# Cross-attention and router FFN on one core: where scores and transposed probabilities stand in PSUM, and the order of a slot's work

## The reference, cut to what matters

```python
def attention(query, key, value, position_ids, mask, Wq, Wk, Wv, Wo):   # 32 batches of 64 rows, E = 512
    q = (query @ Wq)  # 32 heads of D = 128
    k = (key @ Wk)    # 8 key/value heads, each for 4 heads of q
    v = (value @ Wv)
    q, k = rope(q), rope(k)
    scores = where(mask == 0, -1e9, q @ k.T / sqrt(D))
    return (softmax(scores) @ v) @ Wo

def ffn(x, weight, bias, gate_w, in_channel_scale, out_channel_scale):
    routing = softmax(x @ gate_w.T)
    return x * (routing @ in_channel_scale) @ sign(weight).T * (routing @ out_channel_scale) + bias

x = x + attention(layernorm(x), ctx, ctx, pos, mask, Wq, Wk, Wv, Wo)
x = x + ffn(layernorm(x), ...)
```

## Time and profile before

| | us |
|---|---|
| median of 3 runs (1306.85 to 1307.28) | 1307.17 |
| the profiled execution | 1309.06 |
| its span | 1307.2 |
| PE busy | 1192.8 (91%) |
| DVE busy | 842.7 (64%) |
| POOL busy | 722.0 (55%) |
| ACT busy | 554.0 (42%) |
| mean granted clock of PE | 0.978 |

### The profile page before, as it was taken

How to read it: one execution, slowest core, us unless ns; L and a number is a source line. 1 busy time by engine, 2 the same in 40 slices (tenths; PEclk the granted TensorE clock), 3 DMA queues, 4 the chain that set the end, 5 groups by cost and what they waited for, 6 DMA issues and landing times.

```text
span 1307.2 us, 23826 instructions
## 1 busy us (share of the span) xinstructions
PE 1192.8 (91%) x7636; PEld 957.9 (73%) x7636; DVE 842.7 (64%) x1367; ACT 554.0 (42%) x1768; POOL 722.0 (55%) x593
## 2 busy tenths in 40 slices
PE   5799999999999999998999999999999999999977
PEld 4577777777777777776777777777777777777755
DVE  6667666666676666666666666656666666666644
ACT  3344444444434444443444444444444354344422
POOL 4566654554665554655455665545565655565424
PEclk8799999999999999999999999999999999999977
DMA  8233332222322222332322322323222222232100
GB/s 212 66 101 101 92 95 77 80 76 75 110 82 73 72 80 64 115 95 86 87 63 65 97 75 77 96 62 101 81 82 80 66 72 64 72 89 73 57 1 33
DMA packets 136924, 106.04 MB, mean 81 GB/s; under 512 B 12776, under 2 KB 111080, under 8 KB 136864
## 3 DMA queue, kind: packets, MB, share of 16 engines
q1 hardware_dynamic: 131488, 94.78, 25.0%
q10 hardware_dynamic: 4608, 8.39, 1.9%
q0 software_dynamic: 768, 2.10, 0.5%
HBM read 101.05 MB, written 4.19 MB: 81 GB/s over the span
## 4 chain that ended last, share of the span: by engine, by line
PE 66%; DVE 15%; ACT 7%; issue 7%; POOL 2%; ACTq 1%; DMA 1%; SPq 1%; DVEq 1%; POOLq 0%
PE chunk L1001 18%; PE chunk L1003 16%; PE chunk L1002 16%; ACT probs L529 5%; PE o_ps L1073 5%; PE sc_ps L1048 4%; PE tr_ps L990 3%; DVE scores L724 2%; DVE oT_lo L707 2%; DVE neg_max L729 1%; DVE acc L714 1%; DVE f_tile L813 1%; PE aux L1151 1%; DVE swp L773 1%; POOL y L430 1%
## 5 line engine op out<-in xcount | busy, mean ns | idle before, releaser
L396 POOL TENSOR_TENSOR w_lo<-raw,w_hi 128x512 fp32r<-128x512 f32 x192 | 256.6, 1343 | 473.1 <-ACT w_hi L495 472.6
L773 DVE TENSOR_TENSOR swp<-chunk,sinT 64x512 f32<-64x512 f32 x320 | 220.3, 689 | 42.6 <-PE chunk L1003 37.5
L529 ACT ACTIVATE probs<-scores,neg_max 128x64 f32<-128x64 f32 x512 | 171.0, 335 | 149.6 <-DVE neg_max L729 149.6
L1001 PE MATMUL chunk<-wo_hi,oT_hi 128*128 128x512 f32 x512 | 210.2, 411 | 1.8 <-issue 1.8
L1001 PE MATMUL chunk<-xT_hi,w_hi 128*128 128x512 f32 (+1 forms) x512 | 208.2, 407 | 0.2 <-DVE kT L775 0.2
L1003 PE MATMUL chunk<-wo_hi,oT_lo 128*128 128x512 f32 x512 | 201.6, 394 | 0.0
L1002 PE MATMUL chunk<-wo_lo,oT_hi 128*128 128x512 f32 x512 | 201.1, 393 | 0.0
L1002 PE MATMUL chunk<-xT_lo,w_hi 128*128 128x512 f32 (+1 forms) x512 | 200.9, 392 | 0.0
L1003 PE MATMUL chunk<-xT_hi,w_lo 128*128 128x512 f32 (+1 forms) x512 | 200.3, 391 | 0.0
L403 POOL TENSOR_TENSOR qT<-qT,swp 128x512 f32<-128x512 f32 x128 | 165.9, 1296 | 46.8 <-DVE qT L775 46.8
L396 POOL TENSOR_TENSOR wo_lo<-raw,wo_hi 128x512 fp32r<-128x512 f32 x132 | 170.2, 1290 | 20.6 <-ACT wo_hi L495 20.6
(11 more groups left out here) (266 smaller groups left out, 2005.2 us busy)
## 6 DMA issues: line engine op xcount, KB each, us to landing
raw<-in_L_xattn_Wo SPq DMA_DIRECT2D x132, 256.0 KB, 2.6
raw<-in_L_xattn_Wq SPq DMA_DIRECT2D x128, 256.0 KB, 2.7
raw<-in_L_xattn_Wk SPq DMA_DIRECT2D x32, 256.0 KB
raw<-in_L_xattn_Wv SPq DMA_DIRECT2D x32, 256.0 KB
acc<-in_x ACTq DMA_DIRECT2D x16, 256.0 KB, 2.8
c_tile<-in_ctx SPq DMA_DIRECT2D x12, 256.0 KB, 3.0
x_tile<-in_x SPq DMA_DIRECT2D x12, 256.0 KB, 3.5
result<-y ACTq DMA_DIRECT2D x12, 256.0 KB, 2.1
```

The source lines that it names most:

```text
L396: nc.gpsimd.tensor_tensor(lo, raw[:, n % RING, :], hi.bitcast(F32), ALU.subtract).then_inc(wsplit_lo, 1)
L529: last = nc.scalar.activation(probs[:, d, bass.ts(k, S)], scores[:, 2 * d + k // 4, bass.ts(k % 4, S)], ACT.Exp, bias=neg_max[:, d, k:k + ...
L773: last = nc.vector.tensor_tensor(swp[to, k, :], bank[of, :], sinT[to, here], ALU.mult)
L1001: nc.tensor.matmul(bank, a_hi, b_hi, start=i == 0, stop=False)
```

## The change

- PSUM: duo 0 has `sc_ps` for its scores and then for its transposed probabilities, duo 1 has `tr_ps` in the same way (`DUO_BANK`). V's transposes go to the first bank of `o_ps` (`V_BANK`), the transposed rope rows to the second (`TABLE_BANK`) in place of `aux`.
- Waits of PE: `v_rows` waits for the last `out_lo` of the slot before (was: the last `pT_lo_split`). `scores_of(s, d)` waits for the slot before's `pT_lo_split` of the same duo (was: the `soft_a` before it). `probs_T` waits only for its own probabilities. `values(s, 0)` now waits for `v_ok` and, in an intake slot, `rope_ok`; `values(s, 1)` waits for the two `out_lo` of `values(s, 0)` as before. `t_rows` no longer waits for `c_lo`; `t_x` waits for `c_lo` in place of `rope_ok`.
- PE's order in a slot: out_proj 0, v_rows, scores 0, scores 1, (t_context, t_f), out_proj 1, 2, 3, project 0, probs_T 0, probs_T 1, (t_rows, t_x, t_logits), project 1, values 0, (t_route), project 2, (t_in_scales), project 3, (t_out_scales), values 1, project 4, (t_product), project 5.
- The orders of ACT, DVE and POOL are rewritten to fit. No instruction is added or removed, and none changes its shape.

```diff
+        DUO_BANK, V_BANK, TABLE_BANK = [sc_ps, tr_ps], o_ps[0], o_ps[1]
...
(POOL, slot)
                 if s.proj:
                     rope_sum(s, 0)
+                    rope_sum(s, 1)
                     split_lo(s, 5)
                     split_lo(s, 6)
-                    rope_sum(s, 1)
                     split_lo(s, 7)
                     rope_sum(s, 2)
                 if s.ffn:
                     xs_lo_split(f[0], in_slot)
                 if s.proj:
+                    rope_sum(s, 3)
                     split_lo(s, 8)
-                    rope_sum(s, 3)
                     split_lo(s, 9)
                     rope_sum(s, 4)
...
(ACT, slot: a residual load, the store and the ends are as before)
-                if s.attn:
-                    v_in_rows(s)
                 if s.proj and not s.first_proj:
                     split_hi(s, 0)
                     split_hi(s, 1)
+                if s.attn:
+                    v_in_rows(s)
+                if s.proj:
+                    split_hi(s, 2)
                 if s.intake:
                     c_split(*t)
+                if s.ffn:
+                    f_transposed(f[0], in_slot)
                 if s.attn:
                     exp_duo(s, 0)
-                if s.proj:
-                    split_hi(s, 2)
+                    exp_duo(s, 1)
+                    pT_hi_split(s, 0)
                 if s.intake:
                     rope_tables(*t)
-                if s.ffn:
-                    f_transposed(f[0], in_slot)
-                if s.attn:
-                    exp_duo(s, 1)
-                if s.intake:
                     x_split(*t)
-                if s.attn:
-                    pT_hi_split(s, 0)
                 if s.ffn:
                     router_exp(f[0], in_slot)
-                if s.attn:
-                    pT_hi_split(s, 1)
+                if s.proj:
+                    split_hi(s, 3)
+                    split_hi(s, 4)
                 if s.number == SLOTS:
                     for n in range(HG):
                         split_hi(s, n)
-                if s.proj:
-                    split_hi(s, 3)
-                    split_hi(s, 4)
-                if s.attn:
+                if s.attn:
+                    pT_hi_split(s, 1)
                     out_hi(s, 0)
                     out_hi(s, 1)
...
                 if s.proj:
                     split_hi(s, 5)
                     split_hi(s, 6)
-                if s.attn:
-                    out_hi(s, 2)
-                    out_hi(s, 3)
-                if s.proj:
                     split_hi(s, 7)
...
                 if s.ffn:
                     xs_split(f[0], in_slot)
+                if s.attn:
+                    out_hi(s, 2)
+                    out_hi(s, 3)
+                if s.ffn:
                     out_scales(f[0], in_slot)
...
(DVE, slot, as it reads now)
+                    f_norm(*f, in_slot)
                 if s.wo:
                     add_out(s, 0)
                 if s.attn:
                     v_lo_split(s)
+                    soft_a(s, 0)
+                    soft_a(s, 1)
                 if s.intake:
+                    c_lo_split(*t)
                     x_norm(t[0])
                 if s.wo:
                     add_out(s, 1)
                 if s.attn:
                     soft_b(s, 0)
                 if s.wo:
                     add_out(s, 2)
+                    add_out(s, 3)
+                if s.attn:
+                    soft_b(s, 1)
...
+                if s.proj:
+                    rotate(s, 0)
+                if s.ffn:
+                    router_max(f[0], in_slot)
+                if s.attn:
+                    pT_lo_split(s, 0)
                 if s.intake:
                     x_lo_split(*t)
                 if s.ffn:
                     routing(f[0], in_slot)
+                if s.proj:
+                    rotate(s, 1)
                 if s.attn:
                     pT_lo_split(s, 1)
+                if s.ffn:
+                    route_lo(f[0], in_slot)
+                if s.attn:
                     out_lo(s, 0)
                     out_lo(s, 1)
                 if s.proj:
+                    rotate(s, 2)
+                if s.ffn:
+                    scale_in(f[0], in_slot)
...
+                if s.proj:
+                    rotate(s, 3)
                 if s.attn:
                     out_lo(s, 2)
                     out_lo(s, 3)
...
(PE, waits)
                 pe.wait_ge(vT_ok, s.U)
                 if not s.first_attn:
-                    pe.wait_ge(pT_l, (s.U - 1) * DUOS)
+                    pe.wait_ge(o_lo, (s.U - 1) * PAIRS)
...
                 pe.wait_ge(roped, s.U * KQ)
-                if not (s.first_attn and d == 0):
-                    pe.wait_ge(masked, n)
+                if not s.first_attn:
+                    pe.wait_ge(pT_l, n - DUOS + 1)
...
                 if d == 0:
                     pe.wait_ge(v_ok, s.U)
+                    if s.intake:
+                        pe.wait_ge(rope_ok, jobs_of(s)[0][0] + 1)
                 else:
                     pe.wait_ge(o_lo, 2 * n)
```

More of the change, by code:

```diff
@@ L867, in slot @@
                     add_out(s, 2)
-                if s.attn:
-                    soft_a(s, 1)
-                if s.intake:
-                    x_lo_split(*t)
-                if s.wo:
                     add_out(s, 3)
                 if s.attn:
-                    pT_lo_split(s, 0)
-                if s.ffn:
-                    router_max(f[0], in_slot)
-                if s.attn:
                     soft_b(s, 1)
-                if s.ffn:
-                    routing(f[0], in_slot)
                 if s.first_proj:
@@ L890, in slot @@
                 if s.proj:
-                    rotate(s, 1)
-                if s.ffn:
-                    route_lo(f[0], in_slot)
-                if s.attn:
-                    out_lo(s, 2)
-                    out_lo(s, 3)
+                    rotate(s, 2)
                 if s.ffn:
                     scale_in(f[0], in_slot)
-                if s.proj:
-                    rotate(s, 2)
                 if s.first_proj:
@@ L904, in slot @@
                     rotate(s, 3)
+                if s.attn:
+                    out_lo(s, 2)
+                    out_lo(s, 3)
                 if s.ffn:
@@ L1047, in scores_of @@
                                 queries = slice(at * P + a * S, at * P + (a + 1) * S)
-                                last = nc.tensor.matmul(sc_ps[a * S:(a + 1) * S, bass.ts(place, S)],
+                                last = nc.tensor.matmul(DUO_BANK[d][a * S:(a + 1) * S, bass.ts(place, S)],
                                                         qT[:, hp, queries], kT[:, bass.ts(at, S)], start=True, stop=True)
@@ L1066, in values @@
                 pe.wait_ge(pT_l, n + 1)
-                if not (s.first_attn and d == 0):
+                if d == 0:
+                    pe.wait_ge(v_ok, s.U)
+                    if s.intake:
+                        pe.wait_ge(rope_ok, jobs_of(s)[0][0] + 1)
+                else:
                     pe.wait_ge(o_lo, 2 * n)
@@ L1166, in slot @@
                     scores_of(s, 0)
+                    scores_of(s, 1)
                 if s.intake:
                     t_context(t)
-                if s.wo:
-                    out_proj(s, 1)
-                if s.intake:
-                    t_rows(t)
                 if s.ffn:
@@ L1175, in slot @@
                 if s.wo:
+                    out_proj(s, 1)
                     out_proj(s, 2)
-                if s.attn:
-                    scores_of(s, 1)
-                if s.intake:
-                    t_x(t)
-                if s.wo:
                     out_proj(s, 3)
+                if s.proj:
+                    project(s, 0)
                 if s.attn:
                     probs_T(s, 0)
+                    probs_T(s, 1)
+                if s.intake:
+                    t_rows(t)
+                    t_x(t)
                 if s.ffn:
@@ L1187, in slot @@
                 if s.proj:
-                    project(s, 0)
+                    project(s, 1)
                 if s.attn:
-                    probs_T(s, 1)
                     values(s, 0)
-                if s.proj:
-                    project(s, 1)
                 if s.ffn:
                     t_route(f, in_slot)
-                if s.attn:
-                    values(s, 1)
                 if s.proj:
@@ L1207, in slot @@
                     t_out_scales(f, in_slot)
+                if s.attn:
+                    values(s, 1)
                 if s.proj:
```

43 lines of the change are left out of this document (18 added, 25 removed).

## The result

The changed kernel takes 1205.8 us (median of 4 runs, 1205.16 to 1207.55), the kernel before 1307.22 in the same comparison (1306.85 to 1307.34). The ratio is 0.9227, with a 95% interval of 0.9211 to 0.9243: 101.4 us less. The forecast was 1213.5, with a range of 1203 to 1245. The profiled execution took 1205.52, its span is 1203.7 us, the mean granted clock 0.989.

The account below looks back on a forecast made before the run. PE was taken as the bound. Slot gains of 85.2 us plus 3.0 and 5.5 at the ends, 93.7 in all, took the profiled 1309.06 to 1215.4, less 1.9 to the median: 1213.5 us, range 1203 to 1245.

Parts of the forecast that it names:

- The bound: Whole kernel: PE, busy 1192.8 of 1307.2 us, sets the end; the change can gain only where PE stands idle.
- The layout of a slot: Table of starts in a slot on all engines: 33.3 us plain, 34.2 intake, with 0.4 to 2.2 us spare at seams.
- Rival (a): POOL bounds a slot, its eight late instructions taking 1.50 us instead of 1.27: 29 us in all, 1242 us; chance 7%.
- each group of small matmuls costs 0.25 us beyond its own work: On PE between wide blocks: 0.17 us in the first wide block after, some 0.08 at the step to small.
- 0.37 + 1.23 + 0.25: Plain slot's gain: waits for soft_b and out_lo gone, one small-matmul group fewer; 1.85 us, with 2.0 taken.
- Intake: Twelve intake slots: waits for soft_b, out_lo and small ones go, two groups fewer; 3.6 us each, 43.2 in all.
- Slots 1 and 32: The ends: some waits stay; gains of 3.0 us (0 to 5) in slot 1, 5.5 (3 to 6) from slot 32.
- (b): values 0 waits in place of values 1, about 0.8 us in each of 30 slots: 24 us, 1237 us; chance 9%.
- (c): PE's clock falls once per slot in the longer small-matmul stretch, 1.7 us each: 51 us, 1265 us; chance 5%.
- (d): The clock fall in the small-matmul stretch lasts, 7 us a slot: 112 us, 1326 us, slower than before; chance 3%.

Follow-up runs that it names:

- one more group: The changed kernel with probs_T(s, 0) ahead of project(s, 0), so one more group of transposes stands between wide blocks: 1206.93 us, ratio 0.9223.
- `scale_in` first: The changed kernel with scale_in ahead of rotate(s, 2) on DVE in FFN slots: 1200.47 us, ratio 0.9173.
- `pT_lo_split(s, 0)` late: The changed kernel with pT_lo_split(s, 0) behind rotate(s, 1) on DVE: 1338.75 us, ratio 1.0236.

## Why the prediction was right, and where its terms were off

**The bound.** Right. PE's line set the end before and after, and what was gained is PE's time: 114 - 40 = 74 us of idle time, the other 29 overlap, steps between shapes and clock.

**The layout of a slot.** It held to some tenths. `pT_lo_split(s, 0)` ends 0.7 us ahead of `values(s, 0)` in slot 30 (predicted 0.6); `out_lo` 1 ends 2.5 ahead of values 1 (predicted 2.2; one block earlier gave 2.5 again); `scale_in` is late by 0.18 (predicted 0.4, within 0 to 0.8); POOL's last split ends 0.3 ahead of out_proj 0 (predicted 0.4). The last one, in the timeline of POOL, slot 24:

```profile
881.18 1.30 POOL L404 TENSOR_TENSOR qT<-qT,swp 128x512 f32<-128x512 f32 x1 [0.29 <-DVE qT L771]
882.44 2.55 POOL L397 TENSOR_TENSOR wo_lo<-raw,wo_hi 128x512 fp32r<-128x512 f32 x2
```

The two splits of 882.44 end at 884.99, and out_proj 0 starts at 885.33. All of them lie beside DVE instructions with one operand in PSUM, and none is over 1.30 us long. Rival (a) needed 1.50, and nothing of it is seen. The rule of the Trainium skill (GPSIMD Engine Reference, section 8, Key points) names DVE instructions with two SBUF inputs as what POOL contends with. These have one input in PSUM, so by the rule too the splits keep their length, and the trace agrees with 1.30 us at most.

One link was missed. `pT_hi_split(s, 1)` waits until `values(s, 0)` has read the one buffer of `pT_hi`, which the layout had left out. The timeline of ACT in slot 30 shows it:

```profile
1089.47 0.60 ACT L496 ACTIVATE pT_hi<-tr_ps 128x512 fp32r<-128x512 f32 x1 [2.50 <-PE o_ps L1066]
```

It cost nothing, since duo 1's `values` come two blocks later.

**The term that was mis-sized: "each group of small matmuls costs 0.25 us beyond its own work".** This was one number for unlike things. A group of four transposes costs 0.06, a set of 32 scores alone 0.41. And it left out that a wait costs more than its idle time. Each record of a wide matmul is 0.39 us long while one starts every 0.227; the record of the last one before a gap still runs 0.16 us into the gap, and that part is not shown as idle. In a plain slot before, project 0 and the wait behind it took 3.38 us, where the same block between transposes takes 2.85 without a wait (in the kernel with one more group): 0.53 for an idle time of 0.37. Project 1 and its wait took 4.16 against 2.91 now, 1.25 for 1.14. The later kernels agree in the sign: 1.36 for 1.06 with `values(s, 1)` one block earlier (two waits), 0.43 for 0.18 with `scale_in` first. But the surplus is not one number either. It was smallest behind the longest gap, 0.05 for 2.89 in slot 30 with `pT_lo_split(s, 0)` late, and largest at out_proj 0 with POOL's order of before, where 0.41 us were lost and at most 0.18 shown. So a plain slot's 2.15 us are 0.53 + 1.25 of waits and 0.41 of scores, 2.19, and not 0.37 + 1.23 + 0.25. That a plain slot came out at 2.15 with 2.0 taken is in part luck: the groups were priced too high where they are transposes, too low where they are scores, and the waits too low.

**Intake: 48.6 gained, 43.2 predicted.** The typical slot gained 37.81 - 34.22 = 3.6, as taken. The rest is in four slots that were averaged away. Slots 14 and 22 had waits of 0.19 and 0.8 ahead of `t_rows` and `t_x`: 4.7 each. Slot 5 gained 4.0: before, its mean clock was 0.96, behind a gap of 1.63 us at `probs_T(s, 1)`. (The prediction read the 0.99 of this window as no loss.) Slot 15 gained 6.7: it had the 1.81 us gap at out_proj 0 of slot 16, followed by the stretch at clock 0.61. The row of the same instruction after (`issue`: PE waits for nothing that the profile shows):

```profile
565.37 0.49 PE L994 MATMUL chunk<-wo_hi,oT_hi 128*128 128x512 f32 x1 [0.33 <-issue]
```

The gap is 0.33 us and the clock stays up. With the banks alone the gap was 1.92 us and the clock stayed at 1.00 all the same; slot 15 took 40.0 us there against 41.5, so the clock has some 1.5 of the 6.7.

**Slot 0: 3.4 gained, nothing predicted.** Ahead of project 5 stood one gap of 3.8 us, with a lower clock behind it. Now it is two gaps, 1.9 (POOL, `w_lo`) and 1.3 (DVE, `qT`), and in this execution the clock stays at 1.00. PE from 42 to 50 us: before, after, and with POOL's order of before (columns as in the windows above):

```profile
42.00:50.00 8.00, 5.75 (x15) 0.57 0.33 97
```

```profile
42.00:50.00 8.00, 5.96 (x81) 1.00 0.32 101
```

```profile
42.00:50.00 8.00, 6.73 (x70) 0.79 0.26 67
```

With POOL's order of before the one gap of 3.8 us is back, so it is this order that split it; the prediction spoke of it only for the end of a slot. The clock is not the whole gain, and that it stayed up was luck. In three of the seven kernels that have the orders of slot 0 from after, it fell behind the gap of 1.9 us. PE from 38 to 46 us, after and with one more group:

```profile
38.00:46.00 8.00, 6.03 (x24) 1.00 0.34 98
```

```profile
38.00:46.00 8.00, 7.26 (x24) 0.79 0.34 99
```

The second gap is then gone. Counted from the first matmul to the end of the slot, since the first DMA lands at another time in each execution, slot 0 takes 42.4 us before, 40.4 with POOL's order of before, 38.5 after, and 38.8 and 38.5 with one more group and with `scale_in` first, in which the clock fell. So some 1.8 us go with POOL's order, with or without the fall; most of the other 2 fit how long the clock was low behind the gap of 3.8 us (a mean of 0.57 over 8 us against 0.79, which is 1.8 us of work).

**Slots 1 and 32.** The layout had waits of 1.8 and 2.3 us in slot 1, and 1.3 and 2.9 in slot 32. The rows after give 1.7 and 2.0, and 1.18 and 3.14. Slot 1 gained 2.4, not 3.0, and part of that is the clock of this execution: with `scale_in` first slot 1 has the same waits, a mean clock of 0.90 in place of 0.95, and takes 32.7 us in place of 31.5.

**The balance.** The terms gave 93.7 us, the spans 103.5: 3.4 more in slot 0, 5.4 in intake, 0.9 in plain, 0.7 in FFN, 0.6 less in slot 1 and the end. Of these 9.8 the medians show 7.7, since the profiled execution before stood 1.9 above its median and the one after 0.3 below.

**The rivals.** (a), POOL: not so, but its seam is the tightest one: 0.3 us. The order of before or an earlier `values(s, 1)` makes it a wait. (b), `values(s, 0)` late: 0.7 us spare; one rotation more ahead of its split costs 133 us. (c) and (d), the clock: in the slots it read 1.00 after the change, through the longer stretch of small matmuls too. The danger named in (d) is real: a kernel came out slower than before, with a lasting low clock. But there it stood behind a gap of some 3 us in each slot, and not behind that stretch.

**What stays open.** Why the gap at the jump of the loop ahead of slot 16 shrank: 1.81 us before and 1.92 with the banks alone, 0.33 after, 0.26 with one more group, and no row with `scale_in` first. It goes with the orders and not with the banks. One row narrows it: with the later `values(s, 1)` alone it is 0.48 us, so most of it went with this one move; why is not shown. And why the same gap lowers the clock at one place and not at another: 2.89 us in slot 5 and not in slot 30, 1.81 before slot 16 and not 1.92.

## What to carry to other kernels

The new PSUM banks paid only through the order that they permit. So put wide blocks of the bounding engine between each producer and its consumer, and write down for each seam by how much the producer is early. Then look at what hangs on the blocks that moved, since a wait that goes comes back at the next engine's in-order queue (20 us of 33 were kept when only the later `values(s, 1)` was taken over, and 14 us went to POOL when a covering piece moved by one block). Where DVE or POOL has a choice, put first what PE wants first: the one exchange of `scale_in` and `rotate(s, 2)` was worth 5 us.

## What the runs showed of the hardware that was not expected

- A wait of PE costs 0.05 to 0.3 us more than its idle time in the trace; of this 0.16 at most is the last record, which runs on into the gap.
- Four transposes between wide blocks cost 0.06 us beyond their work, 32 matmuls of 128x64 cost 0.41.
- 2.6 us of small f32 matmuls in a row (854.95 to 857.50 in a plain slot) left the granted clock at 1.00. A gap of 2.9 us in each slot brought the mean clock from 0.989 to 0.947 and cost some 42 us beyond the waits, and yet left seven of 30 slots at 1.00.
- Shorter gaps lowered the clock now and then: of the 13 gaps of 1.6 to 1.8 us in the middle of the kernel before, two (slot 5, 1.63; ahead of slot 16, 1.81); of the seven executions with a gap of 1.9 us in slot 0, three. A reading of one execution can thus be off by 1 to 2 us at such a place.
